# Pair work in seven groups of destination blocks instead of eight, in a four-layer graph network

## What is computed

```
agg = segment_sum(edge_vals[:, None] * h[src], dst)     # layer 0: weight-1 edges, then two products with batch norm
f   = segment_sum(edge_weight[:, None] * (h @ W)[src], dst)  # layer 1, twice
y   = segment_sum((norm * (h @ W.T + b))[src], dst) * norm   # layer 2
z   = gat_conv(h, src, dst, ...)                        # layer 3, twice: attention over the edges
```

## Time and profile before

| | us |
|---|---|
| median of three runs | 3895.01 |
| lowest, highest | 3892.2, 3898.1 |
| the profiled execution | 3895.72 |
| its span, first to last instruction | 3894.0 |
| TensorE busy in it | 3403.9 (87%) |
| VectorE busy | 2366.4 (61%) |
| ScalarE busy | 835.4 (21%) |
| GpSimd busy | 651.0 (17%) |
| pair work, first load to the next stage's first product | 260.5 to 893.7 |
| scatter, first to last start | 38.5 to 819.6 |

### The profile page before, as it was taken

How to read it: one execution, slowest core, us unless ns; L and a number is a source line. 1 busy time by engine, 2 the same in 40 slices (tenths; PEclk the granted TensorE clock), 3 DMA queues, 4 the chain that set the end, 5 groups by cost and what they waited for, 6 DMA issues and landing times. The chain is left out here.

```text
span 3894.0 us, 33669 instructions
## 1 busy us (share of the span) xinstructions
PE 3403.9 (87%) x12468; PEld 1931.2 (50%) x12468; DVE 2366.4 (61%) x3072; ACT 835.4 (21%) x1097; POOL 651.0 (17%) x463
## 2 busy tenths in 40 slices
PE   6989855977999999799826999999999999966998
PEld 6877644764554554345513444444444444454444
DVE  9972211335010211334379988998998899857987
ACT  0103212334000000133202222222222222242222
POOL 3788888830000000000000000000000000011000
PEclk9999978998999999899857999999999999987999
DMA  9989967992444344122254222222322232275222
GB/s 359 363 257 277 259 165 175 278 218 69 137 131 133 123 134 154 43 72 60 79 153 129 63 69 84 72 76 65 94 85 70 84 94 74 75 255 178 65 66 65
DMA packets 263804, 525.88 MB, mean 135 GB/s; under 512 B 91593, under 2 KB 152799, under 8 KB 262111
## 3 DMA queue, kind: packets, MB, share of 16 engines
q1 hardware_dynamic: 149561, 443.29, 36.0%
q10 hardware_dynamic: 52480, 60.01, 5.2%
q0 software_dynamic: 61600, 20.44, 4.9%
HBM read 361.99 MB, written 161.67 MB: 134 GB/s over the span
## 5 line engine op out<-in xcount | busy, mean ns | idle before, releaser
L1010 PE MATMUL ps<-R,B 125*128 125x500 f32 x2800 | 1095.2, 542 | 20.8 <-DVE R L1822 13.4
L1010 PEld LDWEIGHTS ps<-R,B 125*128 125x128 f32 x2800 | 503.9, 190 | 592.2 <-issue 544.7
L614 POOL DMA_INDIRECT pairs<-w x400 | 620.9, 1552 | 196.5 <-issue 140.2
L855 PE MATMUL ps<-R,H 125*128 125x500 f32 (+1 forms) x1400 | 554.2, 553 | 35.0 <-DVE R L1595 21.7
L1208 ACT ACTIVATE R<-R,asc 125x1625 f32<-125x1625 f32 (+1 forms) x200 | 320.2, 1601 | 1079.8 <-DVE R L1809 1079.8
L625 POOL DMA_DIRECT2D B<-ct_d x50 | 27.2, 546 | 2696.9 <-PE ps L1010 2571.9
L1822 DVE SCALAR_TENSOR_TENSOR R<-R 125x1625 f32<-125x1625 f32 (+1 forms) x250 | 444.8, 1779 | 0.0
L1809 DVE SCALAR_TENSOR_TENSOR R<-H,asc 125x1625 f32<-125x1625 f32 (+1 forms) x200 | 368.9, 1845 | 115.3 <-PE ps L1017 87.3
L738 PE MATMUL ps<-R,H 125*128 125x375 f32 (+1 forms) x1000 | 314.5, 463 | 117.8 <-DMA R<-pairs 117.8
L855 PEld LDWEIGHTS ps<-R,H 125*128 125x128 f32 x1400 | 258.8, 195 | 316.3 <-issue 313.7
L1684 DVE SCALAR_TENSOR_TENSOR Fb<-R,asc,Fb 125x1625 f32<-125x1625 uint16 (+1 forms) x192 | 353.7, 1842 | 5.5 <-DVE Fb L1684 0.5
(11 more groups left out here) (281 smaller groups left out, 2799.4 us busy)
## 6 DMA issues: line engine op xcount, KB each, us to landing
pairs<-R SPq DMA_DIRECT2D x25, 3200.0 KB
R<-ct_d SPq DMA_DIRECT2D x175, 406.2 KB, 3.2
R<-ct_d SPq DMA_DIRECT2D x175, 375.0 KB, 3.1
R<-pairs SPq DMA_DIRECT2D x25, 2500.0 KB
R<-wt_d SPq DMA_DIRECT2D x50, 812.5 KB, 4.4
R<-wt_d SPq DMA_DIRECT2D x50, 750.0 KB, 4.2
wt_d<-R ACTq DMA_DIRECT2D x13, 1250.0 KB
wt_d<-B ACTq DMA_DIRECT2D x12, 1250.0 KB
```

What stands on the lines that cost most here:

```text
L614: pool.indirect_dma_start(pairs, bass.IndirectOffsetOnAxis(ap=key_u[:, c:c + 1], axis=0), val[:, c, :], None, compute_op=ALU.add)\
L855: last = mm(ps[:, bank, at:at + w], rows[0:Q, j, f * 128:(f + 1) * 128], TL[q % TS][0:Q, o:o + w], start=j == 0 and at == 0, stop=j == NB ...
L1010: last = mm(ps[:, bank, at:at + w], rows[0:Q, j, f * 128:(f + 1) * 128], TT[q % TR][0:Q, o:o + w], start=j == 0 and at == 0, stop=j == NB ...
```

## The change

`SIZES` becomes six groups of four destination blocks and one of one: blocks 20 to 23, before in two groups of two, are one group. The number of units falls from 40 to 35, which is odd, so the two waits of SyncE for all stores count the units of each buffer, 18 and 17.

```
-SIZES = [4, 4, 4, 4, 4, 2, 2, 1]
+SIZES = [4, 4, 4, 4, 4, 4, 1]
...
             for s in range(2):
-                sp.wait_ge(S(f"w_st{s}"), 16 * (len(PUNITS) // 2))
-                sp.wait_ge(S(f"c_st{s}"), 16 * (len(PUNITS) // 2))
+                sp.wait_ge(S(f"w_st{s}"), 16 * len(range(s, len(PUNITS), 2)))
+                sp.wait_ge(S(f"c_st{s}"), 16 * len(range(s, len(PUNITS), 2)))
```

## The result

| | before | after |
|---|---|---|
| median | 3896.1 us (3891.1 to 3898.1, six runs) | 3910.7 us (3906.2 to 3914.0, six runs) |
| ratio, 95% interval | | 1.0043 (1.0031 to 1.0054) |
| profiled execution's span | 3894.0 | 3912.2 |
| pair work ends, next stage begins | 893.7 | 914.3 |
| behind the pair work | 3000.3 | 2997.9 |

What follows compares the result with a forecast made beforehand. The scatter's rounds release the pair work's groups, and its end sets all that follows: start 802.1 + 74.5 + 40.9 = 917.5 us, 23.8 later, so 3895.0 + 23.8 = 3918.8, say 3919 us; range 3909 to 3931.

Steps and rivals of the forecast that it cites:

- The release: Merged group of blocks 20 to 23 waits for 96 scatter rounds instead of 88; TensorE begins it at 802.1 us.
- the early and the late date of the 96 rounds: Start of the merged group: 802.1 us with nearly empty queues, taken; 808 us kept as the late end.
- The group: Merged four-block group takes group 4's own 74.54 us, against 97.91 for ten two-block units; ends at 876.6 us.
- The one-block group: Last group, paced by stores: 2.3, 10.5, 7.3, 8.0, 8.6 and 4.2, together 40.9 us (bounds 38 and 44); 38.08 before.
- The end of the pair work: Pair work ends and the next stage starts at 917.5 us, 23.8 us later than before.
- Behind it: Stretch from the next stage's first product to the end: nothing hides the delay, stays 3000 us.
- The median: Whole kernel: 3895.0 + 23.8 = 3918.8, say 3919 us; this case had chance 0.88.
- Rival 2: Delay absorbed behind the pair work, or the change doesn't reach the schedule: 3895 us; chance 0.04.
- Rival 1: Merged group's rounds already finished when group 4 ends, so no wait: 23.0 us sooner, 3872 us; chance 0.03.
- Rival 3: Merged group gets its last windows only at the scatter's end, four rounds more: 53.5 us later, 3949 us; chance 0.05.
- the confirming signs: New profile: TensorE gap about 44 us, round wait ending near 793, group end near 877, next stage near 917, then 3000 us.

Runs made afterwards that it cites:

- The release without the merge: Kernel before, its two groups of two kept, but the first waits for the 96 rounds of the second: 3931.9 us, ratio 1.0102.
- the experiment without the late release: Changed kernel, but the merged group loads rows of blocks 0 to 3 and is released with group 4 (80 rounds): 3871.5 us, ratio 0.9939 to the kernel before.
- the third series: Changed kernel run again unmodified, beside the kernel before: 3908.8 us against 3896.8, ratio 1.0031.
- three and two: Changed kernel with its last two groups cut as three and two blocks instead of four and one: 3875.9 us, then 3877.5; ratios 0.9953 and 0.9951 to the kernel before.

## Why the prediction was right, point by point

*The release* (802.1 us, from 674.33 + 118.88 + 8.85): TensorE began at 801.53. The load was issued at 792.76 us, 0.45 before the sum. The choice between the early and the late date of the 96 rounds was the right one: with the queues nearly empty they are posted at the scatter's own pace: in the kernel after the load that begins group 4 goes out at 674.10 us, and that of the merged group 118.7 us later. That GpSimd keeps one pace holds for the stretch read, 674.79 to 793.67 us; between 297 and 452 us it lost up to 3.4 us in the unchanged kernels, and this moves all later dates. The release without the merge shows the same date within 3.4 us.

*The group* (74.5): 74.1 us. Taking group 4's own duration, cold start included, was right. What the prediction said beside it, that a four-block unit does not wait for its stores, is true behind a gap only; the experiment without the late release had 23.6 us of such waits.

*The one-block group* (40.9): 38.7 us. Two of its terms, 2.3 and 7.3, are not what the earlier trace rows give (2.49 and 6.68), and no row shown gives them. All six were a little too long: 1.8 for 2.3 to the first evacuation, 10.1 for 10.5, 6.8 for 7.3, 7.5 for 8.0, 8.4 for 8.6, 4.0 for 4.2. The group came out 0.6 us above its duration before: the interval behind the four-block store is 2.0 us longer (10.1 against 8.1), and the others together are 1.4 us shorter. As a mechanism ("paced by stores") the step was too simple: stores issued earlier didn't shorten it, and a store more lengthened an interval by 1.3 to 2.1 us, less than it would in a strict queue.

*The end of the pair work* (917.5, 23.8 us later): 914.28, 20.6 us later; the 2.2 us of the one-block group, the 0.6 of the start and the 0.4 of the group make up the 3.2.

*Behind it* (unchanged, 3000.3): 2997.9 us in the profile, 2.4 us shorter. With the 3.2 of the pair work the 23.8 us of the forecast become 18.2 in this pair of profiles.

*The median* came out 14.6 us higher, for a reason that no term covers: the profiled execution of the kernel after, at 3914.0 us, was the slowest of its six, 3.3 us above their median, and the profiled one of the kernel before was 0.4 below its own. So the mechanism and its dates were right, and the size was too large: 14.6, 29.6 and 12.0 us in the three comparisons, 18.7 on average, against 23.8. The measured 3910.7 us lies 1.7 us above the lower end of the range, and the third series, 3908.8, just below it; that the time fell inside owes something to luck. The upper end holds a slip: 3895 + 35 + 3 is 3933, not 3931.

*Rival 2*, a delay absorbed behind the pair work, falls by the median and by the order of the work: the first matrices from `wt_d` are loaded from 921.87 us on (901.04 before), and their first product starts at 989.20 us, 74.9 us behind the end of the pair work, 73.8 before. The block moved along with its cover, as the prediction said.

*Rival 1*, the case without the wait, was priced at 3872 us and measured 3871.5, but by luck: its group took 82.6 and not 72.1 us, its tail 38.7 and not 40.9, the pair work ended at 878.4 and not 870.7, and the stretch behind had 2994.7 us and not 3000.3. It also left out that the last group has its own release by the last round, some 832 us, which would have held a group that ended sooner. As a rival for the change it falls, by the gap of 43 us. *Rival 3* falls too: the group was released 118.7 us behind group 4, the length of 16 rounds, not of 20.

Of the confirming signs that were named, all but the last came as written: the gap, the single wait ending near 793 us, the group's end near 877 (875.6), the next stage near 917 (914.3); the stretch behind it was not 3000 us but 2997.9.

## What to carry to other kernels

Where a consumer follows a producer group by group, a group's date is that of its last member: merging two groups saves work in the consumer, and costs the whole time until the later member is there if the consumer has nothing else to do. List for each cut when each group is released, when the engine comes free, and what is left after the last release. Here that table, filled from one profile, foresaw both the loss of four and one (+23.8 us forecast, +12 to +30 measured) and, within a few microseconds, the gain of three and two (−12 forecast, −16 and −19 measured), which keeps the gap short and leaves little behind the scatter.

## What the runs showed of the hardware that was not expected

- A second store of 640 rows of 250 B made each interval that waited for it 1.3 to 2.1 us longer than in the kernel after; with the same bytes in 128 rows it was −0.2 to +0.6 us. One profile each.
- Units of four blocks take 16.5 us on average (82.6 / 5) when they run on without a gap beside the scatter, and 14.8 (74.1 / 5) after a gap.
- Issuing the same stores some microseconds earlier went with a scatter that ended at 823.8 us; it ended at 815.9 to 820.6 in five profiles of the kernels before and after.
- The scatter's date moves by 4.7 us between executions of unchanged kernels, and the end of the pair work in the kernel after moves with it (910.9 to 915.8 us).
- The kernel with the two-block groups differs by 15 us between series (3881.6 to 3896.8 us), the one with the merged group by 2.4 (3908.8 to 3911.2).
